# Attention over the 32 best keys: mask, weights and head sum dealt out anew to ScalarE, VectorE and GpSimd

## What is computed

```python
scores = where(vision_mask, Q @ K / sqrt(32), -inf)     # 4 heads x 77 keys for each row
topv, topi = top_k(scores, 32)
attn = zeros_like(scores).at[..., topi].set(softmax(topv))
c_t = (attn.mean(axis=heads) @ V) * text_mask
scale_in, shift_in = split(c_t @ W_film_in + b_film_in)
x1 = layernorm(x) * (1 + gate * scale_in) + gate * shift_in
y = s4d(x1)            # a long convolution over the 1024 rows, done by Fourier transforms
y = y * (1 + gate * scale_out) + gate * shift_out
xt = x + y;  xt = xt + ffn(layernorm(xt));  return layernorm(xt) * g_norm_out + b_norm_out
```

## Time and profile before

| what | value |
|---|---|
| median of 3 runs | 830.08 us (827.86 to 830.58) |
| span of the profiled execution | 837.2 us |
| busy: PE, DVE, POOL, ACT | 685.7, 562.3, 390.7, 303.7 us |

### The profile page before, as it was taken

How to read it: one execution, slowest core, us unless ns; L and a number is a source line. 1 busy time by engine, 2 the same in 40 slices (tenths; PEclk the granted TensorE clock), 3 DMA queues, 4 the chain that set the end, 5 groups by cost and what they waited for, 6 DMA issues and landing times.

```text
span 837.2 us, 10768 instructions
## 1 busy us (share of the span) xinstructions
PE 685.7 (82%) x3380; PEld 383.8 (46%) x3380; DVE 562.3 (67%) x1710; ACT 303.7 (36%) x654; POOL 390.7 (47%) x450
## 2 busy tenths in 40 slices
PE   4879788629899999989897769687696999999971
PEld 3435445524354545444575334232442464657651
DVE  4758876484984848342688799896665595744266
ACT  1555555302738383711224355464011311031210
POOL 4779766035887878742121566877000120212020
PEclk9979978658999999989998789798696999999986
DMA  8920011111222222123970000200100000000003
GB/s 219 390 79 1 1 42 46 60 37 67 76 77 76 77 76 83 70 77 101 334 269 2 1 1 1 101 2 1 50 1 0 1 0 0 2 0 1 1 0 100
DMA packets 33087, 52.77 MB, mean 63 GB/s; under 512 B 8718, under 2 KB 21582, under 8 KB 32776
## 3 DMA queue, kind: packets, MB, share of 16 engines
q1 hardware_dynamic: 28040, 36.75, 12.9%
q0 software_dynamic: 4992, 15.34, 5.4%
HBM read 36.61 MB, written 15.47 MB: 62 GB/s over the span
## 4 chain that ended last, share of the span: by engine, by line
PE 45%; DVE 27%; POOL 9%; ACT 7%; issue 6%; DMA 4%; POOLq 1%; SPq 0%; DVEq 0%; ACTq 0%
PE ps L470 42%; DVE arena L2015 4%; DVE arena L1521 4%; DVE arena L2012 3%; POOL arena L1351 3%; POOL arena L1357 2%; DMA arena<-scr_g 2%; DVE arena L1527 2%; ACT L1147 1%; ACT arena L990 1%; DVE kp L1521 1%; DVE arena L1624 1%; DVE arena L1873 1%; DVE X L1527 1%; ACT L1161 1%
## 5 line engine op out<-in xcount | busy, mean ns | idle before, releaser
L470 PE MATMUL ps<-arena 64*32 64x32 f32 (+10 forms) x2344 | 497.1, 402 | 25.3 <-DVE arena L1810 8.7
L470 PEld LDWEIGHTS ps<-arena 64*32 64x32 f32 (+7 forms) x2344 | 234.3, 155 | 219.4 <-issue 170.7
L990 ACT ACTIVATE arena<-ps 128x512 f32<-128x512 f32 (+4 forms) x252 | 121.4, 493 | 284.4 <-PE ps L470 136.3
L331 POOL TENSOR_SCALAR rstd<-mv 128x1 f32<-128x1 f32 (+2 forms) x30 | 13.7, 458 | 242.3 <-DVE mv L325 191.1
L1873 DVE TENSOR_TENSOR arena<-ps,arena 128x512 f32<-128x512 f32 x39 | 26.9, 689 | 83.6 <-ACT arena L1147 76.5
L1400 POOL DMA_INDIRECT scr_g<-arena,destU x39 | 49.7, 1274 | 43.6 <-DVE arena L1873 34.8
L1391 POOL DMA_INDIRECT arena<-scr_z,idsU x39 | 49.0, 1257 | 22.7 <-PE ps L706 10.9
L2015 DVE MATCH_REPLACE8 arena<-arena 128x77 f32<-128x77 f32 x256 | 54.1, 221 | 0.0
L1147 ACT ACTIVATE arena<-ps 128x512 f32<-128x512 f32 x39 | 23.3, 598 | 81.8 <-PE ps L470 81.5
L1351 POOL TENSOR_TENSOR arena<-arena 128x616 f32<-128x616 f32 x32 | 40.3, 1259 | 24.2 <-DVE arena L1626 22.6
L1284 ACT ACTIVATE arena<-ps,b1p 128x512 f32<-128x512 f32 x32 | 22.0, 687 | 74.7 <-PE ps L470 74.7
(11 more groups left out here) (203 smaller groups left out, 1020.0 us busy)
## 6 DMA issues: line engine op xcount, KB each, us to landing
arena<-in_w1t SPq DMA_DIRECT2D x8, 1024.0 KB, 14.2
arena<-scr_g SPq DMA_DIRECT2D x8, 1024.0 KB, 8.5
X<-in_x SPq DMA_DIRECT2D x2, 1024.0 KB, 5.9
scr_z<-arena SPq DMA_DIRECT2D x4, 512.0 KB, 2.9
arena<-in_c_dftf SPq DMA_DIRECT2D x1, 2048.0 KB, 15.8
arena<-in_L_xattn_W SPq DMA_DIRECT2D x2, 1024.0 KB, 6.3
out<-X SPq DMA_DIRECT2D x16, 128.0 KB, 1.8
scr_k<-arena SPq DMA_DIRECT2D x4, 256.0 KB, 5.3
```

Of the source, the lines that this page charges most:

```text
L470: return pe.matmul(o, l, r, start=first, stop=final)
L990: return a.activation(o, i, ACT.Copy)
```

## The change

The mask is built on ACT, the weights on DVE, the products and the sum over heads on POOL. The statistics of batch 1 are gathered ahead of the loop and its tiles are normalised in two halves (steps 2 and 3). The two folded products are done in POOL's steps 9 and 10, one in each. The closing bias is added to X behind the `stage_end`. The core of the diff:

```diff
-TAKEN = -3.0e38
+TAKEN = -2.0 ** 126
# PE
                         if i == 0:
-                            pe.wait_ge(s["sd_ready"], 2)
+                            pe.wait_ge(s["sd_ready"], 1)
...
                         else:
+                            pe.wait_ge(s["sd_ready"], 2)
                             pe.wait_ge(s["xf_sb"], i)
# ACT
+                        a.wait_ge(s["top_max"], n + 1)
+                        a.activation(smC[:, n % 2, 3, :], top[:, n % 2, :, 0], ACT.Copy, scale=-1.0).then_inc(s["top_neg"], 1)
                         a.wait_ge(s["top_neg"], n + 1)
                         if n >= 2:
-                            a.wait_ge(s["AT_ps"], n - 1)
+                            a.wait_ge(s["attn_ready"], n - 1)
...
-                                a.wait_ge(s["top_full"], n)
+                                a.wait_ge(s["top_full"], 4 * n)
...
-                        a.wait_ge(s["top_full"], n + 1)
-                        if n >= 2:
-                            a.wait_ge(s["ex_sum"], 4 * (n - 1))
                         for h in range(H1):
+                            a.wait_ge(s["top_full"], 4 * n + h + 1)
                             a.activation(topx[:, n % 2, h, :], top[:, n % 2, h, :], ACT.Exp, ...).then_inc(s["ex_sum"], 1)
+                        a.activation(Rk[:, n % 2, :], Rk[:, n % 2, :], ACT.Exp, bias=below[:], scale=128.0 / TAKEN)\
+                            .then_inc(s["ex_sum"], 1)
# POOL, stage C
+                rstd_u(1)
                 for step in range(1, NT + 2):
-                    if step == 3:
-                        rstd_u(1)
...
-                        p.wait_ge(s["ex_sum"], 4 * (n + 1))
-                        own.done(p.tensor_tensor(q_[:, 1, :], q_[:, 0, :], negone[:], ALU.pow))
-                        own.settle()
-                        own.done(p.tensor_scalar(q_[:, 2, :], q_[:, 1, :], tmask[:, n:n + 1], None, ALU.mult))
-                        own.settle()
-                        p.wait_ge(s["exC"], 4 * (n + 1))
-                        p.tensor_tensor(hE, hE, <weight of the head>, ALU.mult).then_inc(s["weighted"], 1)
+                        p.wait_ge(s["exC"], 4 * (n + 1))
+                        p.wait_ge(s["ex_sum"], 5 * n + 5)
+                        own.done(p.tensor_tensor(E, E, Rk[:, n % 2, :], ALU.mult))
+                        own.settle()
+                        p.wait_ge(s["weight_ready"], n + 1)
+                        own.done(p.tensor_tensor(hE, hE, <weight of the head>, ALU.mult))
+                        own.settle()
+                        own.done(p.tensor_tensor(pair, pair, Ex[:, n % 2, 2 * S2:4 * S2], ALU.add))
+                        own.settle()
+                        if n >= 2:
+                            p.wait_ge(s["AT_ps"], n - 1)
+                        p.tensor_tensor(a77[:, n % 2, :], Ex[:, n % 2, 0:S2], Ex[:, n % 2, S2:2 * S2], ALU.add)\
+                            .then_inc(s["attn_ready"], 1)
...
-                    if step == TB + 1:
+                    if step in (TB + 1, TB + 2):
+                        i = step - TB - 1
...
-                        for i, kind in enumerate((ALU.add, ALU.subtract)):
-                            p.tensor_tensor(SD[:, i], *folded(0), kind).then_inc(s["sd_ready"], 1)
+                        p.tensor_tensor(SD[:, i], *folded(0), (ALU.add, ALU.subtract)[i]).then_inc(s["sd_ready"], 1)
...
-                        p.tensor_scalar(xn[:, n % 2, :], U[:, n, :], rstd[:, TB + n:TB + n + 1], None, ALU.mult)\
+                        p.tensor_tensor(xn[:, n % 2, :], U[:, n, :], rstd[:, TB + n:TB + n + 1].broadcast_to([P, D]), ALU.mult)\
...
-                        p.tensor_tensor(X[:, n, :], X[:, n, :], rows[:, BNO, :], ALU.add).then_inc(s["xbE"], 1)
# POOL, behind stage_end, ahead of rstd_E(0)
+                for n in range(NT):
+                    p.tensor_tensor(X[:, n, :], X[:, n, :], rows[:, BNO, :], ALU.add).then_inc(s["xbE"], 1)
# DVE
+                v.wait_ge(s["lnU_rstd"], 1)
+                gather_u(1)
                 for step in range(NT + 1):
-                    if step == 3:
-                        gather_u(1)
-                        norm_u(1, range(TB))
+                    if step in (2, 3):
+                        norm_u(1, range(4 * (step - 2), 4 * (step - 1)))
...
                         if n >= 2:
-                            v.wait_ge(s["ex_sum"], 4 * (n - 1))
+                            v.wait_ge(s["attn_ready"], n - 1)
...                         # in round 1, between max and match_replace
+                            if n and r == 1:
+                                v.wait_ge(s["ex_sum"], 5 * n - 1)
+                                own.done(v.reciprocal(smC[:, 1 - par, 1, :], smC[:, 1 - par, 0, :]))
...                         # in round 0, ahead of the last match_replace
-                                    v.tensor_scalar(smC[:, par, 3, :], top[:, par, :, 0], -1.0, None, ALU.mult)\
-                                        .then_inc(s["top_neg"], 1)
+                                    v.nop().then_inc(s["top_max"], 1)
...                         # the four match_replace of round 3
+                                    ins.then_inc(s["top_full"], 1)
...                         # behind round 1
+                            v.tensor_scalar(smC[:, 1 - par, 2, :], smC[:, 1 - par, 1, :], tmask[:, n - 1:n], None, ALU.mult)\
+                                .then_inc(s["weight_ready"], 1)
...                         # L2026 (ks_done) stands behind round 2 now, not behind round 3
-                    if n < NT:
-                        v.nop().then_inc(s["top_full"], 1)
...
-                        own.done(stt(E, Rk[:, 1 - par, :], TAKEN / 1.5, E, ALU.is_le, ALU.mult))
-                        own.settle()
-                        v.tensor_reduce(a77[:, 1 - par, :], E.rearrange("p (h k) -> p k h", h=H1), AX, ALU.add)\
-                            .then_inc(s["attn_ready"], 1)
```

More of the change, by code:

```diff
@@ L102, in build @@
         trib, onesb = sb("trib", [P, P], BF16), sb("onesb", [P, P], BF16)
-        neghalf, negone = sb("neghalf", [P, 8]), sb("negone", [P, H1])
+        neghalf, below = sb("neghalf", [P, 8]), sb("below", [P, 1])
         mask16, mask32 = sb("mask16", [P, HG]), sb("mask32", [P, H1])
@@ L292, in build @@
             lnC_stats lnC_rstd u_ready uT_ps uT_sb lnU_rstd prepC_ps prepC_sb prepC_v sC_ps sC_read
-            top_neg top_full exC ex_sum weighted xn_ready film_sb attn_ready AT_ps AT_sb film_ps xin_ready maskC bfilm_in
+            top_max top_neg top_full exC ex_sum weight_ready xn_ready film_sb attn_ready AT_ps AT_sb film_ps xin_ready maskC bfilm_in
             dfx_in sd_ready xf_ps xf_sb yf_ready inv_ps hs_sb unfolded fo_ps xt_ready
@@ L1303, in _ @@
             own.done(p.memset(neghalf[:], -0.5))
-            own.done(p.memset(negone[:], -1.0))
+            own.done(p.memset(below[:], -128.0))
             own.done(p.memset(ones[:], 1.0))
@@ L1447, in _ @@
                 p.tensor_tensor(KL[0:1, 0, :], KL[0:1, 0, :], rows[0:1, DSKIP, :], ALU.add).then_inc(s["maskC"], 1)
+                rstd_u(1)
                 for step in range(1, NT + 2):
[L1449 to L1450 removed]
                     if step <= NT:
                         n = step - 1
[L1453 to L1457 removed]
+                        E, pair = Ex[:, n % 2, :], Ex[:, n % 2, 0:2 * S2]
+                        hE = E.rearrange("p (h k) -> p h k", h=H1)
+                        p.wait_ge(s["exC"], 4 * (n + 1))
+                        p.wait_ge(s["ex_sum"], 5 * n + 5)
+                        own.done(p.tensor_tensor(E, E, Rk[:, n % 2, :], ALU.mult))
                         own.settle()
[L1459 removed]
+                        p.wait_ge(s["weight_ready"], n + 1)
+                        own.done(p.tensor_tensor(hE, hE, smC[:, n % 2, 2, :].unsqueeze(2).broadcast_to([P, H1, S2]), ALU.mult))
                         own.settle()
[L1461 to L1463 removed]
+                        own.done(p.tensor_tensor(pair, pair, Ex[:, n % 2, 2 * S2:4 * S2], ALU.add))
[4 more added lines that the diff above has]
+                            .then_inc(s["attn_ready"], 1)
                     if step >= 2:
@@ L2012, in _ @@
                                 own.done(v.max(top[:, par, h, 8 * r:8 * r + 8], hv(cur)[:, h, :]))
+                            if n and r == 1:
+                                v.wait_ge(s["ex_sum"], 5 * n - 1)
+                                own.done(v.reciprocal(smC[:, 1 - par, 1, :], smC[:, 1 - par, 0, :]))
+                                weighed = own.n
                             for h in range(H1):
                                 v.wait_ge(own.sem, before + h + 1)
-                                own.done(v.match_replace(hv(Rr)[:, h, :], top[:, par, h, 8 * r:8 * r + 8],
-                                                         hv(cur)[:, h, :], TAKEN))
@@ L2017, in _ @@
                                 if r == 0 and h == H1 - 1:
```

(27 more changed lines are left out.)

7 lines of the change are left out of this document (removed).

## The result

The changed kernel takes 804.7 us in the median (803.3 to 810.3), the kernel before 829.0 us beside it: a ratio of 0.973, with a 95% interval of 0.970 to 0.977. The forecast was 807.5 us in a range of 800 to 818.

What follows compares the result with a forecast made beforehand. DVE was taken to bound stage C's loop, with PE and ACT's way close behind. Stage C would save 26.6 us and stage D give back 4.0: 22.6 less, 830.1 to 807.5 us, range 800 to 818.

Steps and rivals of the forecast that it cites:

- DVE as the bound, with PE next to it: Stage C's loop: DVE bounds it; after the change DVE, PE and the loop through POOL all give 6.1 to 6.2 us.
- the way over PE and ACT: Stage C's loop, from `attn_ready` to DVE's next-but-one step: 6.9 us long before, giving 6.1 a step after the change.
- DVE's small instructions: DVE's step in stage C: negation goes, reciprocal and multiplication of 4 elements come, net +0.1 us; step 5.9, or 6.2.
- The way of `attn_ready`: Stage C's step: weights, POOL's product and two half sums bring `attn_ready` 5.1 us into the step.
- The start: Stage C up to step 3's first `max`: stall of 4.24 and gathering go, 479.83 becomes 471.4, 8.4 us less.
- Steps 9 to 14: Stage C: steps 9 and 10 save 4.2 us with folded products split, steps 11 to 14 save 4.1.
- Tail: Stage C from step 15 to the end of POOL's last shift: 17.1 us becomes 14.3, 2.8 less.
- drain: End of stage C: POOL's drain, 6.5 us behind its last work, stays as before.
- Stage D: 16 closing additions beside DVE's products make DVE 8.5 to 9 us late; beyond 4.8 slack, 4.0 given back.
- The rival of full collisions: Stage D: each addition stops DVE for its whole 0.72 us, PE 6.8 late, 810.3 us; chance 0.22.
- that of free additions: Stage D: DVE less than 5 us late, additions cost nothing, 26.6 us saved, 803.5 us; chance 0.15.
- The slower rival: Stage C's loop: POOL's products and sums at 1.3 us each, `attn_ready` late every step, 835 us; chance 0.03.

Runs made afterwards that it cites:

- after: The changed kernel with the whole change, run beside the kernel before: 804.7 us, ratio 0.973.
- the new division alone: Changed kernel with closing bias back in POOL's loop, batch 1's norm late and both folded products in one step again: 815.3 us, ratio 0.985 to the kernel before.
- the last kernel: Changed kernel with the closing bias added in stage E's gap and a POOL drain ahead of `rstd_u(0)`: 793.3 us, ratio 0.959 to the kernel before.

## Why the prediction was right, and where not

**DVE as the bound, with PE next to it: right, and shown.** One more reduction lengthens the steps (0.58), one more product of POOL or copy of ACT doesn't. The step came out at 6.09, forecast 6.2: PE's list and DVE's meet there. That the way over PE and ACT gives the same length, as the forecast had it, is not shown by a run of its own.

**DVE's small instructions: right in sum.** The scaling costs 0.27 and the reciprocal 0.16 as rows, against the negation's 0.25; steps without a transform block take 5.76, forecast 5.9. One reading was a little off: before, the first `max` of step 9 begins at 524.00, not at the end of the head sum (524.09). The way of `attn_ready`, 4.8 against 5.1, was right in each term to 0.1.

**The start: 7.2 saved, not 8.4.** The stall of 4.24 went as forecast. The mis-sized terms are in step 2, 8.85 us instead of 7.55. I had said that the transform block's earlier place costs nothing, as its copy ends before round 2 does; here DVE waits 0.66 us for that copy. And the second four norms take 2.08 instead of 1.35. DVE, and PE ahead of the copy, in after:

```profile
456.82 0.42 DVE L2051 TENSOR_TENSOR arena<-ps,arena 128x256 f32<-128x256 f32 x1 [0.66 <-ACT arena L991]
...
458.55 2.08 DVE L336 TENSOR_SCALAR arena<-X,mv,rstd 128x256 f32<-128x256 f32 x4
```
```profile
449.56 0.49 PE L820 MATMUL ps<-ident,arena 128*77 128x128 f32 x1 [4.87 <-POOL arena L1470]
449.85 7.37 PE L470 MATMUL ps<-arena 128*128 128x512 f32 x10
```

I had taken the way over PE from the earlier trace rows, where its ten matmuls take 4.46 us at a clock of 1.00. Behind a wait of 4.87 they take 7.37, and the copy of the block comes late by it. The norms lie beside POOL's shift and normalised tile at 458.74 and 459.50, themselves 0.80 and 0.66 long instead of 0.73 and 0.62; that these slow each other fits, but wasn't tested.

**Steps 9 to 14: 8.3 saved, 8.3 forecast, but not where I put it.** I had the folded products in steps 9 and 10 and their lateness, 1.0, in step 10. They begin at 503.58 and 510.48, which is in DVE's steps 10 and 11; these take 6.04 and 7.29 us instead of 5.76. The lateness is thus 1.8 and not 1.0, and the steps beside it are 0.1 shorter each than forecast. That the sum comes out is luck.

**Tail 2.2, forecast 2.8; drain 6.49, as forecast.** The drain was rightly taken as unchanged. Why it takes so long I did not ask, and there lay the largest cheap gain.

**Stage D: -2.9, forecast -4.0: right mechanism, a little mis-sized.** DVE was 7.8 us late, I had 8.5 to 9; the slack was 7.8 - 3.25 = 4.5, I had 4.8. Per addition DVE lost 0.49 us. The Trainium skill, SBUF — State Buffer (Who interferes with whom), gives the shared ports to one of the two engines for its whole instruction and blocks the other. By that rule, an estimate from the 0.72 of the earlier trace rows, DVE would lose 11.5 us and end at 26.2 + 11.5 = 37.7. The trace agrees on the collision but not on the size: DVE ended at 34.0, so product and addition overlap in part. It is POOL that loses most, 1.60 for an instruction of 0.72. The rival of full collisions (810.3) and that of free additions (803.5) both fall by these rows, though 803.5 lies nearer to the measured median, 804.7, than my 807.5: what decides between them is the row, not the total.

**A rival's price.** The slower rival took steps 3 to 14 at 7.1 us on average before; they take (569.1 - 479.8) / 12 = 7.4, so that its case comes to about 831 us and not 835. Nothing else hangs on it.

**The size as a whole.** 22.5 us saved by the table, against 22.6, is closer than the terms deserve and in part luck: 1.2 too much in stage C, 1.1 too much given back in stage D. The medians say 829.0 - 804.7 = 24.4. The 1.9 between them stay open: the only execution of before that has a trace is not one of those that make its median, and had a lower clock.

## What to carry to other kernels

Where an engine is idle inside a step, work moved to it pays even at half the speed, as long as what it hands on comes earlier than before: the new division alone gave 13.2 us in stage C. Work moved out of a loop needs a place where the engine that it collides with waits, not only a place where its own engine is idle: the same 16 additions took 25.65 us and 12.01. And look at every wait of a stage's end for what it pays for: a drain is cheap to move, and a gap of PE can cost again in the clock behind it.

## What the runs showed of the hardware

- A drain of GpSimd ends 0.07 us behind the work ahead of it (0.83 as a row, with a shift of 0.72 in it), and 0.082 us later for each indirect DMA issued since the last drain, long after these have landed.
- Behind waits of PE of 3.25, 4.87 and 6.9 us the granted clock was 0.50 (1.2 GHz) for some time, and ten matmuls of 128x512 took 7.0 to 7.4 us instead of 4.46. So a wait cost again, behind its end: 3 us in stage D where PE bounds it, nothing where PE then waits for DVE. When the clock falls wasn't tried: behind waits of 2.3 us in step 15 it is 1.00 in after and 0.50 in the last kernel.
- DVE's products with two operands in SBUF and GpSimd's additions slow each other: 1.23 to some 1.7 us, and 0.72 to 1.60. One behind the other they would have taken 37.7 us; side by side they took 34.0.
- Up to 4 us between profiled executions of kernels whose stage D is the same (247.5 and 251.3) go with the granted clock there (0.88, 0.78 and 0.83, 0.69). What set it later in stage D wasn't tried.
